# Self scores of a wide attention by a stationary block of ones in four column groups

## The reference, cut to what matters

```python
ik = input_seq @ Wk + bk;  mk = state_seq @ Wk + bk
iv = input_seq @ Wv + bv;  mv = state_seq @ Wv + bv
q = jnp.einsum('bmd,hdp->bhmp', state_seq, Wq) + bq[None, :, None, :]
inp_score = jnp.einsum('bhmp,bsp->bhms', q, ik)
self_score = jnp.sum(q * mk[:, None], axis=-1, keepdims=True)
score = jnp.concatenate([self_score, inp_score], axis=-1)
attn = jax.nn.softmax(score / jnp.sqrt(p_), axis=-1)
v_in = jnp.einsum('bhms,bsp->bhmp', attn[..., 1:], iv)
heads = v_in + attn[..., 0:1] * mv[:, None]     # then heads @ Wo + bo
```

## Time and profile before

| | |
|---|---|
| timed executions | 822.15, 824.37 and 828.03 us |
| median | 824.37 us |
| span of the profiled execution, first to last instruction | 827.5 us |
| mean granted clock of TensorE over the span | 0.925 of full |
| the wide attention in it | about 203 to 382 us |

### The profile page before, as it was taken

One profiled execution on the slowest core, in us unless ns is written; L12 is line 12 of the kernel. 1 busy time (PEld: TensorE's weight loads), 2 busy tenths in 40 slices (PEclk: granted clock), 3 DMA queues, 4 the chain that ended last, 5 costly groups with the idle time before them and its releaser, 6 DMA issues. The chain is left out here.

```text
span 827.5 us, 14508 instructions
## 1 busy us (share of the span) xinstructions
PE 728.2 (88%) x4910; PEld 606.0 (73%) x4910; DVE 559.8 (68%) x1478; ACT 415.8 (50%) x1280; POOL 373.3 (45%) x375
## 2 busy tenths in 40 slices
PE   6985899998899999996679999799869999996775
PEld 3654699997899998884568788556658988885664
DVE  6887773455799998885645777658765466666554
ACT  3892344335455555553124777379824456663211
POOL 6753312102566644433212667466440478874001
PEclk9798799999999999998959999859978999999768
DMA  7000011110000000000003445000010231300000
GB/s 275 2 2 26 14 32 46 51 38 13 1 2 1 2 8 1 1 2 1 8 19 110 137 146 175 4 1 2 2 45 22 91 115 65 101 13 0 1 1 26
DMA packets 14276, 33.11 MB, mean 40 GB/s; under 512 B 1744, under 2 KB 5864, under 8 KB 13952
## 3 DMA queue, kind: packets, MB, share of 16 engines
q1 hardware_dynamic: 14208, 32.26, 11.5%
HBM read 31.63 MB, written 0.62 MB: 39 GB/s over the span
## 5 line engine op out<-in xcount | busy, mean ns | idle before, releaser
L1213 PE MATMUL banks<-input_hi,weights_in_lo 128*128 128x512 f32 x296 | 125.7, 425 | 16.4 <-PEq L1588 11.7
L1213 PE MATMUL banks<-input_lo,weights_in_hi 128*128 128x512 f32 x296 | 120.4, 407 | 0.0
L1213 PE MATMUL banks<-input_hi,weights_in_hi 128*128 128x512 f32 x296 | 119.9, 405 | 0.0
L1213 PEld LDWEIGHTS banks<-weights_out,hidden 128*128 128x128 f32 x864 | 101.6, 193 | 11.1 <-issue 8.1
L1213 PE MATMUL banks<-weights_out,hidden 128*128 128x128 f32 x864 | 102.9, 277 | 7.4 <-PEq L1532 6.7
L986 ACT ACTIVATE probabilities<-banks,neg_max 128x128 f32<-128x128 f32 x256 | 90.5, 432 | 15.9 <-DVE neg_max L1916 15.8
L1075 ACT ACTIVATE hidden<-banks,cols 128x512 f32<-128x512 f32 x80 | 54.0, 688 | 73.2 <-ACTq L1073 72.7
L697 POOL TENSOR_TENSOR rstd<-var_eps,neg_half 128x4 f32<-128x4 f32 x24 | 24.9, 1037 | 134.2 <-POOLq L696 114.9
L1213 PEld LDWEIGHTS banks<-input_hi,weights_in_lo 128*128 128x128 f32 x296 | 58.7, 198 | 30.9 <-issue 17.0
L807 POOL TENSOR_TENSOR hidden<-hidden,scratch 128x512 f32<-128x512 f32 x48 | 62.1, 1294 | 19.3 <-ACT hidden L1094 16.7
L1213 PEld LDWEIGHTS banks<-input_hi,weights_in_hi 128*128 128x128 f32 x296 | 58.4, 197 | 13.2
(11 more groups left out here) (274 smaller groups left out, 1755.1 us busy)
## 6 DMA issues: line engine op xcount, KB each, us to landing
scratch<-cw_rows SPq DMA_DIRECT2D x19, 512.0 KB, 3.9
weights_out<-w_in SPq DMA_DIRECT2D x17, 256.0 KB, 2.7
weights_in<-w_in SPq DMA_DIRECT2D x8, 512.0 KB, 3.5
weights_in<-w_in SPq DMA_DIRECT2D x9, 256.0 KB, 2.9
weights_in<-w_in SPq DMA_DIRECT2D x16, 128.0 KB, 2.2
weights_out<-w_in SPq DMA_DIRECT2D x16, 128.0 KB, 2.1
wq<-w1q_in SPq DMA_DIRECT2D x1, 1024.0 KB, 4.8
wo<-w1o_in SPq DMA_DIRECT2D x1, 1024.0 KB, 6.9
```

What stands on the lines that cost most here:

```text
L1213: return pe.matmul(o, l, rh, start=start, stop=stop, **kw)
```

## The change

The four products of the self scores swap their operands: a 128 x 32 block of ones is stationary, `qmk` moves, and each product writes its 128 sums, 32 times over, to one group of 32 partitions of bank 7 (`own_sums`). ScalarE copies the 128 x 128 result to SBUF (`copy_own`), TensorE turns it back (`turn_own`), and VectorE reads every 32nd column. VectorE scales the queries when it evacuates them, so the scale goes from the exponentials and the maxima, and `maxima` has three operations in the place of four. In the lists, the split of the turned heads comes a step earlier (lag 4 for 5 on ScalarE and VectorE, behind `maxima` and `copy_own`), `heads_out` stands first on VectorE, `enter_mlp` on ScalarE stands ahead of `copy_probsT` and `round_headsT`, and `turn_heads` waits until its bank has been read.

```diff
--- before.py
+++ after.py
@@ -189,7 +189,7 @@
         b2_0 = sb("b2_0", [E0, D])
         b2_1 = sb("b2_1", [E1, D])
         ident = sb("identity", [P, P])
-        ones = sb("ones", [P, 1])
+        ones = sb("ones", [P, 32])
         neg_half = sb("neg_half", [P, NB])
         expert_no = sb("expert_number", [P, E1])
         stats = sb("stats", [P, NB, 6])
@@ -202,6 +202,7 @@
         r_wide = sb("inverse_sums_wide", [P, 4, H, DH])
         r_spread = scratch[:, 8:10, :].rearrange("p a t -> p (a t)")
         out_copy = sb("att_unscaled", [D, 2, P])
+        own_copy = out_copy
         row_max = sb("row_max", [P, 2, 4])
         z = sb("exp_sums", [P, 2, H])
         r = sb("inverse_sums", [P, 2, H])
@@ -316,6 +317,9 @@
         heads_q_done = sem("heads_q_done")
         qh_ready = sem("qh_ready")
         wide_scores_done = sem("wide_scores_done")
+        own_sums_done = sem("own_sums_done")
+        context_values_copied = sem("context_values_copied")
+        own_sums_copied = sem("own_sums_copied")
         wide_max_ready = sem("wide_max_ready")
         wide_probs_ready = sem("wide_probs_ready")
         wide_probsT_done = sem("wide_probsT_done")
@@ -1035,6 +1039,11 @@
                     act.wait_ge(headsT_done, n + 1)
                     act.activation(headsT_hi[:, n % 2, :], bank[5][:, :], ACT.Copy).then_inc(headsT_hi_ready, 1)
 
+                def copy_own(it, n):
+                    act.wait_ge(own_sums_done, n + 1)
+                    act.activation(own_copy[:, n % 2, :], bank[7][:, n % 2 * P:n % 2 * P + P], ACT.Copy)\
+                        .then_inc(own_sums_copied, 1)
+
                 def copy_sums(it, n):
                     act.wait_ge(wo_done, 1 + n // 16)
                     act.activation(y_wide, bank[6][:, :], ACT.Copy).then_inc(y_copied, 1)
@@ -1043,7 +1052,7 @@
                     act.wait_ge(wide_max_ready, n + 1)
                     for i in range(4):
                         act.activation(prob[:, 0, 4 * (n % 2) + i, :], b4(1 + n % 2)[:, i, :],
-                                       ACT.Exp, bias=neg_max[:, n % 8, i:i + 1], scale=SC1,
+                                       ACT.Exp, bias=neg_max[:, n % 8, i:i + 1],
                                        accum_out=z[:, 0, 4 * (n % 2) + i:4 * (n % 2) + i + 1])\
                             .then_inc(wide_probs_ready, 1)
                     act.activation(self_exp[:, n % 2, :], self_arg[:, n % 2, :], ACT.Exp)\
@@ -1052,9 +1061,10 @@
                 def enter_mlp(it, n):
                     enter_halves(mlp1)
 
-                pipelined(act, [(take_tokens, (1,), 0), (evacuate_state_keys, (1,), 0), (enter_mlp, (0,), 35),
-                                (round_headsT, range(32), 5), (copy_probsT, range(32), 3),
-                                (exps, range(32), 2), (copy_sums, (15, 31), 6)], 32, 1, st.close)
+                pipelined(act, [(take_tokens, (1,), 0), (enter_mlp, (0,), 35),
+                                (copy_probsT, range(32), 3), (exps, range(32), 2), (copy_own, range(32), 1),
+                                (evacuate_state_keys, (1,), 0), (round_headsT, range(32), 4),
+                                (copy_sums, (15, 31), 6)], 32, 1, st.close)
 
             def router_exp():
                 act.wait_ge(gap_ready, 1)
@@ -1391,14 +1401,20 @@
                     pe.wait_ge(keys_ready, 4)
                     project_tok(w("wv1"), xnT, 4, (1,))
 
-                def self_scores(it, n):
-                    if n > 0:
+                def own_sums(it, n):
+                    if n == 0:
+                        pe.wait_ge(context_values_copied, 2)
+                    else:
                         pe.wait_ge(wide_max_ready, n)
                     pe.wait_ge(qmk_ready, n + 1)
                     for i in range(4):
-                        at = 4 * (n % 2) + i
-                        m = mm(bank[7][:, at:at + 1], qmk[:, n % 2, i, :], ones[:, :])
-                    m.then_inc(wide_scores_done, 1)
+                        m = mm(bank[7][32 * i:32 * i + 32, n % 2 * P:n % 2 * P + P], ones[:, :], qmk[:, n % 2, i, :])
+                    m.then_inc(own_sums_done, 1)
+
+                def turn_own(it, n):
+                    pe.wait_ge(own_sums_copied, n + 1)
+                    pe.transpose(bank[7][:, 256 + n % 2 * P:256 + n % 2 * P + P], own_copy[:, n % 2, :], ident[:, :])\
+                        .then_inc(wide_scores_done, 1)
 
                 def scores(it, n):
                     pe.wait_ge(qh_ready, n + 1)
@@ -1424,6 +1440,8 @@
 
                 def turn_heads(it, n):
                     pe.wait_ge(heads_ready, 4 * (n + 1))
+                    if n > 0:
+                        pe.wait_ge(headsT_ready, n)
                     for i in range(4):
                         t = pe.transpose(b4(5)[:, i, :], heads[:, n % 2, i, :], ident[:, :])
                     t.then_inc(headsT_done, 1)
@@ -1453,10 +1471,11 @@
                     pe.wait_ge(wide_max_ready, 32)
                     transpose_half(0, iv, mlp1.entry_bank(0))
 
-                pipelined(pe, [(queries, range(32), 0), (turn_state, (0,), 0), (self_scores, range(32), 1),
-                               (output, range(32), 6), (turn_heads, range(32), 4), (values, range(32), 3),
-                               (turn_sums, (15, 31), 7), (turn, range(32), 2), (scores, range(32), 0),
-                               (state_rest, (0,), 1), (enter_mlp, (0,), 34)], 32, 1, lambda: None)
+                pipelined(pe, [(queries, range(32), 0), (turn_state, (0,), 0), (own_sums, range(32), 1),
+                               (output, range(32), 6), (turn_heads, range(32), 4), (turn_own, range(32), 1),
+                               (values, range(32), 3), (turn_sums, (15, 31), 7), (turn, range(32), 2),
+                               (scores, range(32), 0), (state_rest, (0,), 1), (enter_mlp, (0,), 34)],
+                          32, 1, lambda: None)
 
             def route(weight, experts, src, at=7):
                 for b in range(NB):
@@ -2021,8 +2040,8 @@
             def wide_attention():
                 def queries(it, n):
                     dve.wait_ge(heads_q_done, n + 1)
-                    dve.tensor_scalar(scratch[:, n % 2, :], bank[0][:, :], col("bq1", n % 16), None, ALU.add)\
-                        .then_inc(qh_ready, 1)
+                    dve.tensor_scalar(scratch[:, n % 2, :], bank[0][:, :], col("bq1", n % 16), SC1,
+                                      ALU.add, ALU.mult).then_inc(qh_ready, 1)
 
                 def state_values(it, n):
                     for half in range(2):
@@ -2042,16 +2061,15 @@
 
                 def maxima(it, n):
                     dve.wait_ge(wide_scores_done, n + 1)
-                    own = bank[7][:, 4 * (n % 2):4 * (n % 2) + 4]
+                    own = bank[7][:, 256 + n % 2 * P:256 + n % 2 * P + P:32]
                     m = row_max[:, n % 2, :]
-                    dve.tensor_reduce(m, b4(1 + n % 2), X_AX, ALU.max).then_inc(st.sem, st.one())
+                    dve.tensor_reduce(m, b4(1 + n % 2), X_AX, ALU.max, negate=True).then_inc(st.sem, st.one())
                     dve.wait_ge(st.sem, st.n)
-                    dve.tensor_tensor(m, m, own, ALU.max).then_inc(st.sem, st.one())
+                    dve.scalar_tensor_tensor(neg_max[:, n % 8, :], own, -1.0, m, ALU.mult, ALU.min)\
+                        .then_inc(st.sem, st.one())
                     dve.wait_ge(st.sem, st.n)
-                    dve.tensor_scalar(neg_max[:, n % 8, :], m, -SC1, None, ALU.mult).then_inc(st.sem, st.one())
-                    dve.wait_ge(st.sem, st.n)
-                    dve.scalar_tensor_tensor(self_arg[:, n % 2, :], own, SC1, neg_max[:, n % 8, :],
-                                             ALU.mult, ALU.add).then_inc(wide_max_ready, 1)
+                    dve.tensor_tensor(self_arg[:, n % 2, :], own, neg_max[:, n % 8, :], ALU.add)\
+                        .then_inc(wide_max_ready, 1)
 
                 def weights(it, n):
                     dve.wait_ge(wide_probs_ready, 5 * (n + 1))
@@ -2116,9 +2134,9 @@
                         dve.sem_inc(norm_tok_ready, 1)
 
                 st.close()
-                pipelined(dve, [(low_headsT, range(32), 5), (heads_out, range(32), 4), (weights, range(32), 3),
-                                (queries, range(32), 0), (state_values, (0,), 2), (maxima, range(32), 1),
-                                (second_tokens, (0,), 2), (residual, (15, 31), 7),
+                pipelined(dve, [(heads_out, range(32), 4), (weights, range(32), 3), (queries, range(32), 0),
+                                (state_values, (0,), 2), (maxima, range(32), 1), (low_headsT, range(32), 4), (second_tokens, (0,), 2),
+                                (residual, (15, 31), 7),
                                 (lambda it, n: split_input(0), (0,), 37),
                                 (statistics, (0, 2), 23), (variance, (0,), 26), (centre, (0, 2), 27),
```

(2 more changed lines are left out.)

## The result

| | median of 7 executions | range |
|---|---|---|
| before | 826.32 us | 822.15 to 828.32 |
| after | 821.08 us | 816.57 to 822.33 |

A forecast was written before the change was run, and what follows sets the result against it. TensorE was taken to set the pace, at 4.95 us a step. Steps 5.7, start 1.0, end 2.8 and clock 2.0 summed to 11.5 us, taking 824.4 to 812.9 us, range 805 to 821.

The forecast's parts named there:

- the slot on TensorE: Self scores in each wide-attention step: groups 0.51 us plus turn back 0.11, so 0.62 against 0.81, a gain of 0.19.
- the 0.11 for the way in: Cost in us of TensorE's change of mode into the column groups, behind the queries' 512 columns.
- The first: Rival: mode switches cost a full drain, slot stays about 0.81 us, only start and end gain; 819.5 us, chance 0.17.
- the third rival: The four groups don't overlap, slot 1.30 us against 0.81, kernel slower at 835 us; chance 0.05.
- a whole record for each: Bound on the slot: 0.27 us for each way in and out, slot 0.85, a loss of 0.04 a step.
- the new waits: TensorE's `turn_own` waits for ScalarE's `copy_own`; ready after 3.1 us, reached after 3.75, so covered by 0.6.
- The start: Line 2051's removal brings back some 1.5 us, `turn_own` waits 0.5; gain 1.0, between 0 and 2.
- The end: `heads_out` first on VectorE, last output 3 us earlier, `copy_own` chain takes 0.2; gain 2.8, between 1.5 and 3.5.
- 30 steps by 0.19: Gain of TensorE's shorter self-score slot over the wide attention's steps: 5.7 us.
- the clock, plus 2.0 forecast: With the 3.1 us wait gone, TensorE's clock holds at the attention's end: 2.0 us gained, 0 if it falls.
- Worth nothing in the steady steps: VectorE loses 0.7 us a step, but TensorE sets the pace, so no time is gained there.
- Beyond room: VectorE's lighter step gives only room: 4.63 us falls to about 3.95 against TensorE's 4.76.

The follow-up runs named there:

- swap_old_order: The kernel after with the places of before in VectorE's and ScalarE's lists, new self sums kept; ratio to before 0.9916.
- order_only: The kernel before with the new places in VectorE's and ScalarE's lists alone, old self scores kept; ratio to before 1.0032.
- vector_only: The kernel before with VectorE's three operations for the maxima, scaled queries and exponentials without a scale alone; ratio to before 0.9973.
- after_four_ops: The kernel after with the four operations of the maxima and the scaling of before; ratio to before 1.0001.
- groups_twice: The kernel after with the four products of the self sums issued twice, 16 passes for 8; one execution, regular step 4.93 us.

## Why the prediction was wrong

**Right: the slot on TensorE.** Predicted 0.62 us against 0.81, measured 0.09 + 0.36 + 0.02 + 0.11 = 0.58; the step went from 4.95 to 4.72, forecast 4.76. That the groups overlap, that the mode costs 0.1 to 0.17 each way and that the pace is TensorE's alone was read from rows of another stage and held. One reading was not of the same thing: the 0.11 for the way in came from a step out of products of 32 rows, not into column groups; that it lies near the measured 0.09 is luck. The first and the third rival are refuted. The Trainium skill, TensorEngine Tiling (Array Packing), Key Properties, says that a switch of the mode drains TensorE; the trace agrees that it costs something, 0.09 us on the way in and 0.15 on the way out, and a whole record for each, as I had priced that rule, it does not cost.

**Right: the new waits, in the regular steps.** `turn_own` never waits in them. It does at the start, 0.40, 0.40 and 1.36 us for units 0, 1 and 2. The start gained 2.0 in all, of which its regular share is about 1 and the rest the 1.0 that I had put down; the waits at `turn_own` are 2.2 in sum where I had 0.5, so that its parts were off.

**The end: the way was right, the size off.** 2.8 predicted for the earlier `heads_out`, 3.3 measured, but of two parts. From the last self scores to `heads_out` it is 12.76 us in before and 10.52 in after, 2.2 gained: GpSimd's product ends 0.45 later behind the last self sums (10.13 for 9.68), and the split of the unit before keeps VectorE from `heads_out` for another 0.4. The other 1.1 lies between `heads_out` and the mark, where the last output and the turned sums now run at the high clock (from the output's start to ScalarE's copy 1.01 for 1.60, from there on to the residual 1.34 for 1.81); it belongs to the clock.

**The failed step: "30 steps by 0.19".** The prediction had looked at fifteen steps without a wait and took the gain for all. The sum has no term for the steps around GpSimd's inverse roots, though the trace of before shows one wait of 1.25 us there. The new list on VectorE puts the 0.68 us split ahead of the variances, a step shorter by 0.23 leaves less time for them, and the roots stand ahead of the products that TensorE wants. The two steps there grew from 11.4 to 14.0 us, and with the one in the middle three irregular steps from 17.8 to 20.5: 2.7 lost where three times 0.19 was forecast to be gained, 3.3 short. Moving the roots, and nothing else, brought back 4.5 us of attention and 0.5% of the kernel: this cause is shown.

**The mis-sized term: the clock, plus 2.0 forecast.** The clock held at the end of the attention, as forecast; it gained the 1.1 us just named and, behind the mark, nothing. In after, TensorE has the MLP's first products done early and then waits 1.83 us for VectorE (before: 0.47):

```profile
379.95 0.50 PE L1223 MATMUL banks<-input_hi,weights_in_lo 128*128 128x512 f32 x1 [1.83 <-DVE hidden L2241]
```

From the mark to the next the MLP took 13.85 us before and 13.86 after. And then it lost: the second half's 32 products took 5.39 us in place of 3.81. Of after, then of before, one product record each (start, duration, engine, line):

```profile
395.82 5.39 PE L1223 MATMUL banks<-weights_out,hidden 128*128 128x128 f32 x32 [2.90 <-PEq L1551]
```

```profile
404.78 3.81 PE L1213 MATMUL banks<-weights_out,hidden 128*128 128x128 f32 x32 [2.92 <-PEq L1532]
```

with, in after, the windows ahead of them

```profile
390.00:394.00 4.00, 2.92 (x13) 2.06 (x11) 3.66 (x10) 2.06 (x3) 1.02 (x1) 1.00 0.00 0
394.00:398.00 4.00, 2.18 (x10) 2.21 (x11) 2.67 (x13) 0.00 (x0) 0.85 (x1) 0.72 0.00 0
```

and in before the same work, 9 us later:

```profile
399.00:403.00 4.00, 2.86 (x13) 2.05 (x11) 3.70 (x10) 2.06 (x3) 1.02 (x1) 1.00 0.00 0
403.00:407.00 4.00, 2.22 (x20) 2.25 (x21) 2.63 (x13) 0.00 (x0) 0.89 (x1) 1.00 0.01 4
```

TensorE's busy time in both pairs is the same to 0.06 us and the clock fell in one and not in the other. These 32 products take 3.81 us in all five traces with the old places and 5.14 to 6.75 in all eight with the new ones; one of each, swap_old_order and order_only:

```profile
397.74 3.81 PE L1223 MATMUL banks<-weights_out,hidden 128*128 128x128 f32 x32 [2.92 <-PEq L1551]
```

```profile
407.86 5.39 PE L1214 MATMUL banks<-weights_out,hidden 128*128 128x128 f32 x32 [2.93 <-PEq L1535]
```

With the old places the clock is low at the end of the attention (in swap_old_order 0.50 from 371 to 379) and 1.00 in these products; with the new ones it is 1.00 at the end of the attention and falls in the products. So it is shown that the new places bring the fall; why it comes, and what would keep the clock up in both, wasn't tried. The clock's term is then 1.1 gained and 1.6 lost, minus 0.5 for plus 2.0.

The MLP took 31.71 us in before and 33.65 in after, 1.9 longer, and 0.35 of that isn't the clock. VectorE waits there once for its own result:

```profile
408.19 0.87 DVE L1840 BATCH_NORM_STATS2 stats<-x_tok 128x6 f32<-128x128 f32 x4 [0.46 <-DVE x_tok L1866]
```

In before it doesn't:

```profile
415.22 0.87 DVE L1821 BATCH_NORM_STATS2 stats<-x_tok 128x6 f32<-128x128 f32 x4
```

The wait stands in all six traces with VectorE's shorter maxima and in none of the other seven, though this code is the same in all; its cause is open.

**The account.** 11.5 forecast, less 3.3 for the irregular steps (0.6 of it their share of the forecast gain, 2.7 the loss), less 2.5 for the clock, less 0.6 at the end (2.2 for 2.8), less 0.35 for VectorE's wait in the MLP, plus about 1.0 in the start and the regular steps (0.23 for 0.19 each): 5.8, which is what the marks give.

**VectorE's part was half wrong.** "Worth nothing in the steady steps" is confirmed by vector_only. "Beyond room" was not priced: in the steps at the start, around the extra work for the next block and at the end, the short maxima are worth 4.1 to 5.4 us of attention, as much as the groups' 4.8 in 21 steps; after_four_ops, which has the groups and all else of the change, gained nothing at all.

## What to carry to other kernels

A gain per step holds only for steps that look like the one you costed: list every step of the loop with its start-to-start time first, and give each one that is longer than the rest its own line in the sum, above all where an engine's list holds a one-off wait ahead of work that others are waiting for. When an engine's list is reordered, ask what one-off stage of the next block is behind the moved operation. A higher clock or a faster engine in a stretch that another engine gates is worth nothing there. Measure an edit to the end of the stage behind it: here the new places gained 1.7 us in their own stage and lost 1.6 in the next.

## What the runs showed of the hardware

A product of a 128 x 32 stationary operand and 128 moving columns in four-byte floats is two passes; with four column groups in turn it cost 0.053 us (0.21 us for the eight passes that groups_twice adds), against 0.22 for two full-width passes at 0.11 each. In after the way into the groups cost 0.09 us behind 512 moving columns and the way out 0.15.

The granted clock of TensorE fell after the wait of 2.88 us (after, 0.66 from 333 to 337) and 2.52 us (order_only, 0.74 from 341 to 345), and also in vector_only after one of 1.05 us (0.71 from 337 to 341); it stayed at 1.00 after 2.29 us (swap_old_order) and after 1.25 us (before). The length of the one wait ahead doesn't decide it by itself.
